# An attention and mixture-of-experts layer on one core: negated queries, a new order of the batch stage, expert weights loaded in the first batch

## What is computed

```python
mod = (_silu(L0_c) @ L0_wmod).reshape(B, 6, 1, -1)        # sa, ca, ga, sb, cb, gb
h = _layernorm(x) * (1 + ca) + sa
x = x + ga * attn(h)       # 16 heads of 16; softmax over 4 sinks and a window of 128; q @ k.T * scale, scale = 1/4
h = _layernorm(x) * (1 + cb) + sb
# moe(h): top 2 of 16 by sigmoid(h @ gate_w.T), their shares times 2.5
routed = sum over the two experts of  share * (silu(h @ w_gate[e]) * (h @ w_up[e])) @ w_down[e]
shared = silu(h @ ws_gate) * (h @ ws_up) @ ws_down
x = x + gb * (routed + shared)
```

## Time and profile before

| | |
|---|---|
| median of 3 runs (lowest to highest) | 323.49 us (322.05 to 323.55) |
| the profiled execution, its span | 324.01 us, 322.2 us |
| PE busy | 264.7 us, 82% |
| DVE busy | 231.9 us, 72% |
| POOL busy | 202.7 us, 63% |
| ACT busy | 164.5 us, 51% |
| moved by DMA | 59.78 MB, mean 186 GB/s |

### The profile page before, as it was taken

The page is one execution under the profiler, slowest core; times in us unless marked ns, Lnnn a source line. Parts: engine busy times, 40 slices in busy tenths (PEclk is TensorE's granted clock), DMA queues, the critical chain, the costliest instruction groups (busy, mean ns, idle before and its releaser), DMA issues.

```text
span 322.2 us, 5982 instructions
## 1 busy us (share of the span) xinstructions
PE 264.7 (82%) x1665; PEld 208.4 (65%) x1666; DVE 231.9 (72%) x900; ACT 164.5 (51%) x518; POOL 202.7 (63%) x255
## 2 busy tenths in 40 slices
PE   3899998898999869978977999999999999983000
PEld 3274476766766556746745989899999988872000
DVE  0566788998799868997899755645554778876790
ACT  4043653278226923458124565566665766755440
POOL 6712316848884766738754777566666678867780
PEclk9999999999999999999997999999999999998555
DMA  7929401144734618922265996555558888848993
GB/s 258 346 76 336 154 2 49 69 116 117 210 82 150 196 66 281 247 63 84 83 194 176 236 216 202 161 168 168 176 173 231 256 262 269 276 139 289 333 372 137
DMA packets 41436, 59.78 MB, mean 186 GB/s; under 512 B 5092, under 2 KB 29880, under 8 KB 41404
## 3 DMA queue, kind: packets, MB, share of 16 engines
q1 hardware_dynamic: 34312, 39.91, 43.8%
q0 software_dynamic: 6528, 17.90, 16.1%
q10 hardware_dynamic: 564, 1.59, 1.4%
HBM read 33.57 MB, written 25.80 MB: 184 GB/s over the span
## 4 chain that ended last, share of the span: by engine, by line
PE 41%; DVE 22%; DMA 15%; issue 7%; SPq 5%; POOL 5%; ACT 3%; DVEq 0%; POOLq 0%
PE bank L1268 14%; PE bank L926 7%; PE bank L1278 6%; DMA p_win<-slots 4%; POOL slots L612 3%; DMA slots<-h_sb,slot_i 3%; PE bank L1088 3%; SPq L381 2%; DMA slots<-pads 2%; DVE h_sb L1411 2%; DVE st L1385 2%; PE bank L969 2%; DMA ht<-in_L_attn_x_dram 2%; DMA ys<-pt_win,row_i 2%; PE bank L1063 2%
## 5 line engine op out<-in xcount | busy, mean ns | idle before, releaser
L612 POOL DMA_INDIRECT slots<-h_sb,slot_i x64 | 63.6, 993 | 32.6 <-DVE slot_i L1482 17.1
L1268 PE MATMUL bank<-ht,v_wide 128*128 128x128 f32 x576 | 77.2, 277 | 0.4 <-DVE xs L1433 0.4
L1268 PEld LDWEIGHTS bank<-ht,v_wide 128*128 128x128 f32 x576 | 71.0, 194 | 0.8 <-DVE xs L1433 0.6
L1782 DVE TENSOR_TENSOR act_t<-bank,sg 128x128 f32<-128x128 f32 x72 | 20.9, 290 | 38.9 <-ACT sg L875 38.0
L670 POOL DMA_INDIRECT ys<-y_more,row_i x36 | 35.1, 974 | 18.9 <-ACT y_more L703 15.2
L703 ACT ACTIVATE ht<-bank 128x256 f32<-128x256 f32 x104 | 39.6, 381 | 13.2 <-PE bank L926 12.7
L670 POOL DMA_INDIRECT ys<-pt_win,row_i x36 | 35.0, 973 | 15.7 <-ACT pt_win L703 10.4
L1278 PE MATMUL bank<-w_dn,act_t 128*128 x144 | 43.4, 383 | 1.0 <-DVE act_t L1782 1.0
L926 PE MATMUL bank<-ident,p_win 128*128 128x128 f32 x198 | 36.0, 277 | 5.4 <-ACT p_win L746 1.9
L1122 PE MATMUL bank<-w_route,ht 128*128 128x272 f32 x128 | 36.0, 404 | 2.2 <-DVE act_sb L1423 1.2
L926 PEld LDWEIGHTS bank<-ident,p_win 128*128 128x128 f32 x198 | 25.8, 142 | 18.1 <-issue 7.2
(11 more groups left out here) (263 smaller groups left out, 513.0 us busy)
## 6 DMA issues: line engine op xcount, KB each, us to landing
p_win<-slots SPq DMA_DIRECT2D x67, 129.0 KB
slots<-pads SPq DMA_DIRECT2D x28, 129.0 KB
xs<-in_L_attn_x_dram SPq DMA_DIRECT2D x3, 1024.0 KB
wmod_sb<-ys SPq DMA_DIRECT2D x12, 256.0 KB, 4.8
w_gu<-ys SPq DMA_DIRECT2D x10, 256.0 KB, 3.3
mod_bc<-mod_rows_out SPq DMA_DIRECT2D x4, 512.0 KB, 5.7
w_dn<-in_L_ffn_w_down_dram SPq DMA_DIRECT2D x1, 2048.0 KB, 11.8
h_sb<-ys SPq DMA_DIRECT2D x8, 256.0 KB, 3.8
```

Of the source, the lines that this page charges most:

```text
L612: pool.indirect_dma_start(out=slots, out_offset=bass.IndirectOffsetOnAxis(ap=slot_i[:, k, j:j + 1], axis=0), in_=h_sb[:, j, :], in_offset= ...
L1268: last = mm(bank[2 + k % 2][:, half * P:(half + 1) * P], w_now[:, k, c, half * M:(half + 1) * M], ht[:, k, c, :], start=(c == 0), stop=(c ...
L1782: v.tensor_tensor(act_t[:, k, :], bank[2 + k % 2][:, P:2 * P], sg[:, k, :], ALU.mult)\
```

## The change

- **Signs.** ACT copies the queries times -SCALE instead of plainly, so that the logits come out negated and scaled, and the mask is filled with +1e30. Maxima become minima: `less_sink` is now the reduction over the sinks itself, `less_max` a plain minimum of two tiles, and DVE's multiplication at L1352 is gone in all four batches.
- **Loads.** The four loads of w_gate and w_up wait for 4 to 7 tiles of h (in batch 0) instead of 10 to 19 (batches 1 and 2), the load of w_down for 9 (first tile of batch 1) instead of 22. The twelve pad writes, which stood in a row behind it, wait for one tile each, 12 to 23 (batch 1, T3, to batch 2, T6).
- **Order.** DVE's `activation`, `chosen` and `norm_stats` are cut into parts, and the parts, PE's and ACT's steps stand in a new order; POOL does one scaling after a scatter instead of before it. A semaphore of its own, `counts`, tells PE that the experts' counts are ready, where DVE and PE waited for `rt_ch`.

The core of the diff:

```diff
             for n, w in enumerate((w_gate, w_up)):
                 for c in range(C):
-                    sp.wait_ge(S["h_ready"], TPB + 2 + 3 * (n * C + c))
+                    sp.wait_ge(S["h_ready"], 4 + n * C + c)
...
-            sp.wait_ge(S["h_ready"], TPB + 2 + 3 * 2 * C)
+            sp.wait_ge(S["h_ready"], TPB + 1)
...
             for s in range(SPARE):
                 r = (NE * CAP + s) * P
+                sp.wait_ge(S["h_ready"], TPB + 4 + s)
                 sp.dma_start(slots[r:r + P, :], pad_rows(NE + s)).then_inc(S["pad_dmas"], 16)
...
-                if 0 < b < B - 1:
-                    scale(b + 1, 0)
                 if b > 0:
                     scatter(2)
...
+                if 0 < b < B - 1:
+                    scale(b + 1, 0)
...
-                copy(qt[:].rearrange("p c n -> p (c n)"), bank[4][:, 0:D]).then_inc(S["at_qs"], 1)
+                act.activation(qt[:].rearrange("p c n -> p (c n)"), bank[4][:, 0:D], ACT.Copy, scale=-SCALE)\
+                    .then_inc(S["at_qs"], 1)
...
                 h_copy(b, 2)
+                at_exp(b, 1)
                 if b == 0:
                     small_out_t()
-                at_exp(b, 1)
                 at_exp(b, 2)
...
+                    down(b, 1, b == 0)
+                act_tr(b, 2, b == 0)
                 at_logits(b, 1)
-                if b > 0:
-                    down(b, 1, b == 0)
                 gate_up(b, 2, b == 0)
-                act_tr(b, 2, b == 0)
...
-                at.done(v.tensor_reduce(m_sink[:], ls, AX.X, ALU.max))
-                at.done(v.tensor_scalar(less_sink[:], m_sink[:], -SCALE, None, ALU.mult))
+                v.tensor_reduce(less_sink[:], ls, AX.X, ALU.min).then_inc(S["at_ch"], 1)
+                at.n += 1
...
+            def counted(half):
+
+                dve.wait_ge(S["masks"], part_no(half, GROUP) + 1)
+                rt.done(v.tensor_reduce(mask_sum[:], mask_b[:].rearrange("p t e -> p e t"), AX.X, ALU.add))
+                v.tensor_tensor(counted_b[:, half + 1, :], counted_b[:, half, :], mask_sum[:], ALU.add)\
+                    .then_inc(S["counts"], 1)
...
                 at_sink_max(b, at)
                 at_less_max(b, 0, at)
                 if b > 0:
                     dve.wait_ge(S["y_ps"], b * TPB - 1)
                     ranked(b * GPB - 1)
+                at_bias(b, 0, at)
...
+            add_y(B, 1)
             expert_table(0)
-            add_y(B, 1)
-            ex_weights(2, e[2])
             expert_table(1)
             add_y(B, 2)
+            ex_weights(2, e[2])
```

More of the change, by code:

```diff
@@ L745, in at_exp @@
                     h = 4 * g + i
-                    last = act.activation(p_win[:, h, :], bank[4 + g % 2][:, i * P:(i + 1) * P], ACT.Exp, scale=SCALE,
+                    last = act.activation(p_win[:, h, :], bank[4 + g % 2][:, i * P:(i + 1) * P], ACT.Exp, scale=-1.0,
                                           bias=less_max[:, h:h + 1])
@@ L803, in _ @@
                 if b > 0:
-                    second_keys(b, range(3, CH))
+                    second_keys(b, range(3, 5))
+                h_copy(b, 0)
+                if b > 0:
+                    second_keys(b, range(5, CH))
                     own_values(b)
                 centre(b, 2)
+                tanh(b, 1)
                 centre(b, 3)
-                tanh(b, 1)
                 if b > 0:
@@ L1147, in rank @@
                 pe.wait_ge(S["masks"], part_no(half, lo) + 1)
+                if half > 0:
+                    pe.wait_ge(S["counts"], half)
                 pe.wait_ge(S["y_added"], added)
@@ L1194, in _ @@
                 tr(b, 2)
+                if b == 0:
+                    small_out_t()
                 at_logits(b, 2)
@@ L1216, in _ @@
                 down(b, 4, b == 0)
-                at_values(b, range(0, H // 2))
+                at_values(b, range(0, 4))
+                at_values(b, range(4, 8))
                 rank(b * GPB, 0, GROUP, b * TPB + 2)
-                at_values(b, range(H // 2, H))
+                at_values(b, range(8, 12))
+                at_values(b, range(12, 16))
                 gate_up(b, 5, b == 0)
@@ L1386, in norm_stats, with norm_sums @@
                     ln.n += 1
+            def norm_sums(b, n, ln):
+                r = range(TPB)[normed(b, n)]
                 dve.wait_ge(S["ln_ch"], ln.n)
@@ L1450, in chosen, with columns @@
                     .then_inc(S["masks"], 1)
+            def columns(half, lo=0, hi=GROUP):
+                b, g = divmod(half, GPB)
+                n = hi - lo
+                first = half * GROUP + lo
+                r = slice(g * GROUP + lo, g * GROUP + hi)
                 for col, src in ((D, token2[:, ds(first, n)]), (D + 1, top_if[:, lo:hi, 0])):
@@ L1456, in chosen @@
                 rt.n += 1
-                if hi == GROUP:
-                    dve.wait_ge(S["masks"], part + 1)
-                    rt.done(v.tensor_reduce(mask_sum[:], mask_b[:].rearrange("p t e -> p e t"), AX.X, ALU.add))
-                    rt.done(v.tensor_tensor(counted_b[:, half + 1, :], counted_b[:, half, :], mask_sum[:], ALU.add))
+            def counted(half):
[3 more added lines that the diff above has]
+                    .then_inc(S["counts"], 1)
             def ranked(half, lo=0, hi=GROUP):
@@ L1712, in _ @@
                     at_norm(b + 1, at)
-                activation(b, 4)
-                chosen(b * GPB)
-                add_y(b, 4)
-                h_tile(b, 5, first)
-                ranked(b * GPB)
+                activated(b, 4)
+                gated_up(b, 4)
+                top_two(b, 4)
                 if b == 0:
@@ L1721, in _ @@
                     norm_stats(b, 3, ln)
+                add_y(b, 4)
+                chosen(b * GPB)
+                columns(b * GPB)
+                counted(b * GPB)
+                h_tile(b, 5, first)
+                if b == 0:
+                    norm_sums(b, 3, ln)
+                ranked(b * GPB)
                 placed(b * GPB)
@@ L1741, in _ @@
                     norm_stats(b, 2, ln)
-                activation(b, 6)
+                if b == B - 1:
+                    activated(b, 6)
+                norm_sums(b, 2, ln)
+                if b + 1 < B:
+                    activated(b, 6)
+                gated_up(b, 6)
+                top_two(b, 6)
                 add_y(b, 6)
```

101 lines of the change are left out of this document (70 added, 31 removed).

## The result

The changed kernel takes a median of 317.42 us (316.76 to 318.38, 4 runs) against 323.38 us (322.05 to 323.55, 4 runs) for the one before: 6.0 us less. Runs over 1.5% above the fastest of their kernel are left out of such ratios. The forecast was 318.4 us, with a range of 315.0 to 322.2. The profiled execution took 316.81 us, its span is 315.0 us, 7.2 us less than before.

A forecast was written before the change was run, and what follows sets the result against it. PE bounds the expert stage, PE and DVE are both near full in a batch, and batch 2 also waits for scatters. Terms -3.3 - 0.4 - 1.8 + 0.4 + 0 = -5.1 us give a 318.4 us median, range 315.0 to 322.2.

The forecast's parts named there:

- The sum: All parts' gains and costs over the whole kernel: -5.1 us, a median of 318.4 us.
- part 2: Loads moved into batch 0 hold its scatters, so T0 of batch 1 waits until 62.7 us; costs 0.8 us.
- part 4: Batches 1 to 3: fewer DVE steps make `slot_i` earlier; -0.6 us a batch, -1.8 in all.
- Part 1: Batch 2: without loads and rows of pads, its two waits (2.89 and 0.43 us) go; -3.3 us.
- they get nothing until q1 is empty: Batch 0: scatters stay held until SP's queue q1 runs out of load data, some 61 us.
- Part 3: Batch 0's new order brings DVE to T0 of batch 1 1.2 us sooner, of which 0.4 remain.
- ACT's exchange: Batch 0: group 1's exponentials ahead of `sm_ot` start earlier, shortening DVE's wait for group 3's logits; -0.7 us.
- The expected wait for `xs<-o_g`: Batch 0: DVE waits for all four `xs<-o_g` ahead of `norm_stats(0,3)`; nothing, or 0.4 us in the ends.
- PE's work and `rden` follow `slot_i`: Batches 1 to 3: PE's chain and DVE's `rden` move earlier with `slot_i`; -0.6 us a batch.
- Part 5: Spread pads in batches 1 and 2 delay awaited scatters, 0.2 us a batch, +0.4; w_down's load counted in the ends.
- rival C: Scatters get turns beside batch 0's loads, so T0 of batch 1 doesn't wait; -5.9 us, 317.6 us; chance 0.10.
- Part 6: Transition to the expert stage, whose first tile behind the pads waits for the last pad: 0, ends ±0.3 us.

The follow-up runs named there:

- the second profile: The changed kernel profiled again, nothing altered, in the session of the follow-up runs; ratio 0.986 to the kernel before.
- the last of the three steps: Changed kernel with two buffers for gated down weights, pads off T3 and T4, POOL's scaling for T2 held until T1 of h; ratio 0.982.

## Why the prediction was right, and where not

- **The sum** was right: 318.4 forecast, 317.4 measured, and by the ratio a gain of 5.0 us for 5.1. In part that is luck: the 0.8 us that part 2 puts at T0 weren't lost, and the batch's gain of part 4 is half of the 0.6 us in batch 1.
- **Part 1 (batch 2's waits)** was right in kind and size: -3.84 us for the whole batch, -3.7 forecast; of the two waits 2.9 us are gone, 3.3 forecast. The loads alone bring 3.45 of it. What it didn't see is that the order alone takes 2.2 us from the same waits.
- **Part 2 (scatters held in batch 0)** was wrong: no 0.8 us are lost at T0. The step that failed is "they get nothing until q1 is empty". It rested on the earlier trace rows, three microseconds with no packet of the scatters. That they were held in these is true, for some 3.4 us, and as long in the run with pads in a row; but then they get in while the load still has data. Beside the loads of batch 0 they land after 5.3 to 7.5 us in all runs with the loads there, and that is before T0 needs them; the 5.5 us of the earlier trace rows would have said so. What T0 had to spare was little: 1.2 us in the changed kernel, 0.2 with the loads alone, 0.3 with loads in pieces. This was rival C, with a chance of 0.10. The Trainium skill's rule (DMA: Bandwidth & Descriptors, Queues, rings and completion order), that an engine goes round the queues, agrees with the packets of both queues in 50 to 61 us, and not with the 3.4 us in which a scatter was held and one queue alone had packets. What decides when a scatter's turn comes was not found: cutting the loads didn't change it. Whether the pads in a row held scatters by their number, their bytes or their direction (writes to memory, not loads) wasn't tested.
- **Part 3 (batch 0)** had the right sum, DVE ready 1.2 us sooner, measured 1.33, but not the right reason. ACT's exchange, put at 0.7 us, is worth nothing in the changed kernel and 0.38 us in the kernel before; the signs, put at 0.3, are worth 0.39 us there. The rest is left for PE's and DVE's order, not tested apart. The expected wait for `xs<-o_g` is there, 0.20 us.
- **Part 4 (0.6 us a batch)** was over-sized as a batch's gain. In batch 1 `slot_i` does end 0.61 us earlier after T0 (7.47 us for 8.08), as forecast, but `rden` starts only 0.39 earlier (22.14 for 22.53), and the batch is 0.29 shorter. The signs alone give nothing in that batch. The step that failed is "PE's work and `rden` follow `slot_i`". PE's free time of 2.7 us didn't help: the chain, DVE's until 70.2 us before, is now PE's from 63.5 to 85.8 us, and part of what DVE gains becomes DVE's idle time, as at the second `place` of batch 1 (0.93 us for 0.61). The place of the wait was right: with `wsd_gated` taken out of it, batches 2 and 3 lose 0.53 us more. The 0.29 us are of one profile; in the second one the same batch took 35.17 us.
- **Part 5 (pads)** came out in the first profile, 0.16 and 0.40 us at T4, 0.2 each forecast. It isn't a fixed price: in the second profile T4 of batch 1 waited for 1.29 us, over the end of 0.5, with a pad issued just ahead of its last scatter. The price of the row that the spread pads replace was not asked, and is the largest number here: 9.3 us in one batch, 5.65 of it at one tile.
- **Part 6 (transition)**: T7 of batch 3 comes 8.0 us earlier, the first expert tile behind the pads 7.5, the end 7.2. Nearly 0.8 us are lost, inside what the last pad's landing varies by (6.08 to 7.89 us in the two profiles of the changed kernel).

Between the forecast's -5.1 us and the profile's -7.2 lie 0.95 us ahead of batch 0, which are not the change's, 0.9 us in batch 0 (the stall that didn't come, 0.8) and 0.5 us from batch 3 on to the pads, less 0.3 us behind them and small differences in batches 1 and 2. The 0.5 us have a likely source that the forecast didn't look for: before, two DVE instructions ahead of and at T1 of batch 3 took 0.66 us for 0.17 and 0.90 for 0.48, beside POOL's scaling.

## What to carry to other kernels

Look for a stage in which a store's landing is awaited late or by nobody, and put the big loads there; what a load costs is the stall of whoever waits for a store of another queue beside it, so read how much time that one has to spare. Here a dozen small writes in a row behind a big load cost more than the load, and the stall cost more than its length, since PE came out of it at half its clock. Taking instructions from an engine helps only if the engine that it works in turn with can follow: the chain names that engine, and its remaining wait is the next thing to take. Compare stretches between like tiles in profiles where runs spread more than the parts of a change are worth, but not on one profile alone: the same batch of the same program took 33.78 and 35.17 us.

## What was not expected of the hardware

Some DVE instructions that start within some tenths of POOL's scaling (128x256) take longer: T1 of h 1.05 us instead of 0.48, `less_max` 0.55 instead of 0.16, `slot_i` 0.56 instead of 0.17. Eight that are over 0.15 us longer than their like stand in the batches' trace of the kernel before, 3.3 us in all; seven in the changed kernel, 2.2 us; four in the last of the three steps, 1.5 us. They end just behind POOL's instruction, as if they waited for it to be over: `less_max`, `slot_i` and `counted_b` 0.03 to 0.06 us behind, T1's h 0.28. One pair of the changed kernel, in batch 0:

```profile
47.90 0.72 POOL L618 TENSOR_TENSOR scaled<-scaled,mod_bc 128x256 f32<-128x256 f32 x1
48.09 0.56 DVE L1522 CAST slot_i<-slot_f 128x8 int32<-128x8 f32 x1
```

Which of the two is late hangs on hundredths. At T1 of batch 1 DVE started first in either case: with 0.04 us between the starts DVE was the loser, with 0.06 us POOL. The Trainium skill (SBUF — State Buffer, Who interferes with whom) has it that DVE and POOL share a pair of ports that one of them holds for a whole instruction, for DVE instructions with two inputs in SBUF too. The row of T1, which has such inputs, agrees in that one of the two is held. Why DVE was held although it had started first, the rows don't show.
